# A two-layer edge network on one core: the column sums of the first pass taken by VectorE before one matmul, and a third of a one-column product moved forward

## What is computed

```python
h = maximum(_layernorm(x), 0)
m = concatenate([h[src], bcol[src], edge_attr]) @ W1 + b1      # E x 256, bcol is 0
m = relu(batchnorm(m, g1, be1))                                # statistics over all E rows
agg = segment_sum(m, dst) / maximum(count(dst), 1)             # N x 256
h2 = concatenate([h, bcol, agg]) @ W2 + b2                     # N x 385
h2 = relu(batchnorm(h2, g2, be2))
out = x + relu(h2 @ W3 + b3)
```

## Time and profile before

| | |
|---|---|
| median of 3 runs | 3194.51 us (3186.86 to 3200.58) |
| profiled execution: its own time, its span | 3181.97 us, 3180.2 us |
| busy: PE, PEld | 2441.9 us (77%), 914.3 us (29%) |
| busy: DVE, ACT, POOL | 1393.9 us (44%), 969.7 us (30%), 1749.7 us (55%) |
| first pass, about 145 to 2430 us of the span | 2285 us |
| second pass, about 2430 to 3075 us | 645 us |
| TensorE clock granted, mean | 0.856 |

### The profile page before, as it was taken

How to read it: one execution, slowest core, us unless ns; L and a number is a source line. 1 busy time by engine, 2 the same in 40 slices (tenths; PEclk the granted TensorE clock), 3 DMA queues, 4 the chain that set the end, 5 groups by cost and what they waited for, 6 DMA issues and landing times. The chain is left out here.

```text
span 3180.2 us, 34295 instructions
## 1 busy us (share of the span) xinstructions
PE 2441.9 (77%) x12138; PEld 914.3 (29%) x12138; DVE 1393.9 (44%) x2299; ACT 969.7 (30%) x1601; POOL 1749.7 (55%) x1850
## 2 busy tenths in 40 slices
PE   4666767657767777777777677777867999999998
PEld 3412112112212222222222122222213433444448
DVE  4422212234323333322333233333223899999878
ACT  3322212112212221222122122212213655655546
POOL 6466666666666666666666666666664222222220
PEclk8888778778878888888888888888876999999999
DMA  8466656666656666666666566566664999999965
GB/s 237 155 210 215 212 194 224 209 221 239 216 194 227 212 213 207 218 204 207 216 229 208 190 223 218 195 228 220 212 206 150 337 350 350 345 343 345 341 238 162
DMA packets 270622, 740.85 MB, mean 233 GB/s; under 512 B 46391, under 2 KB 98661, under 8 KB 270448
## 3 DMA queue, kind: packets, MB, share of 16 engines
q1 hardware_dynamic: 189152, 525.28, 46.2%
q0 software_dynamic: 78432, 212.46, 22.4%
q10 hardware_dynamic: 2864, 0.86, 0.1%
HBM read 501.63 MB, written 236.81 MB: 232 GB/s over the span
## 5 line engine op out<-in xcount | busy, mean ns | idle before, releaser
L621 POOL DMA_INDIRECT sums<-P_d,late x1581 | 1496.5, 947 | 796.4 <-issue 453.3
L1052 DVE TENSOR_TENSOR sums<-psum,sums 128x1024 f32<-128x1024 f32 x396 | 479.0, 1220 | 1524.2 <-remote 823.9
L1351 PE MATMUL psum<-late,sums 128*128 128x512 f32 x1660 | 950.3, 687 | 255.2 <-issue 168.4
L709 ACT ACTIVATE sums<-sums 128x1024 f32<-128x1024 f32 x416 | 437.7, 1054 | 1720.7 <-remote 988.0
L1294 PE MATMUL psum<-sums,ones 128*32 128x512 f32 x830 | 486.5, 667 | 117.8 <-issue 70.2
L1351 PEld LDWEIGHTS psum<-late,sums 128*128 128x128 f32 x1660 | 315.4, 210 | 888.6 <-issue 728.0
L1297 PE MATMUL psum<-sums,ones 128*32 128x512 f32 x830 | 497.9, 676 | 59.5 <-issue 58.6
L1296 PE MATMUL psum<-sums,ones 128*32 128x512 f32 x830 | 494.5, 676 | 36.5 <-issue 35.9
L1295 PE MATMUL psum<-sums,ones 128*32 128x512 f32 x830 | 488.7, 670 | 28.8 <-issue 28.6
L1095 DVE TENSOR_TENSOR late<-late,psum 128x1024 f32<-128x1024 f32 (+1 forms) x407 | 482.6, 1212 | 34.3 <-DMA late<-m_d 32.5
L650 POOL TENSOR_TENSOR late<-dst_f,iota 128x384 f32<-128x384 f32 (+1 forms) x139 | 115.1, 829 | 379.4 <-PE psum L1463 375.3
(11 more groups left out here) (215 smaller groups left out, 2012.0 us busy)
## 6 DMA issues: line engine op xcount, KB each, us to landing
m_d<-sums SPq DMA_DIRECT2D x415, 512.0 KB
late<-m_d SPq DMA_DIRECT2D x406, 512.0 KB, 5.5
sums<-in_ea_main SPq DMA_DIRECT2D x103, 512.0 KB
sums<-P_d,late POOLq DMA_INDIRECT x1581
P_d<-sums SPq DMA_DIRECT2D x24, 512.0 KB
nodes<-in_x SPq DMA_DIRECT2D x24, 256.0 KB
late<-in_x SPq DMA_DIRECT2D x24, 256.0 KB, 3.1
out<-late SPq DMA_DIRECT2D x24, 256.0 KB, 2.4
```

What stands on the lines that cost most here:

```text
L621: pool.indirect_dma_start(out=m_s[s][0:r, k * L:(k + 1) * L], out_offset=None, in_=P1_d, in_offset=bass.IndirectOffsetOnAxis(ap=idx[0:r, G ...
L709: act.activation(q_s[g % Q_SLOTS][0:r, 0:w], m_s[g % M_SLOTS][0:r, 0:w], ACT.Square).then_inc(s_q, 1)
L1052: dve.tensor_tensor(m_s[s][0:r, 0:w], ps_m[place_m[g]][0:r, 0:w], m_s[s][0:r, 0:w], ALU.add).then_inc(s_m, 1)
L1351: ins = pe.matmul(ps_m[place_m[g]][:, 2 * i * L:2 * (i + 1) * L], ea[:, i * P:(i + 1) * P], W1c[:, :], start=True, stop=g not in xg_no, sk ...
```

## The change

`stats(g)` of a whole group becomes one matmul. DVE gets `tile_sums(g)`: it sums the four tiles of m to one 128 x 256 tile, and the four tiles of squares to another, side by side, and PE takes the column sums of these 512 columns. `odd_rows(b, 0)` leaves the second pass and stands behind the counts of the first, one block at every other count. Buffers: two for squares instead of three, two new ones for the tile sums; the statistics now lag four groups instead of three. POOL waits for `s_sums` (DVE has read the buffer) instead of `s_st`.

```diff
-Q_SLOTS = 3
+Q_SLOTS = 2
+SUM_SLOTS = 2
+SUM_LAG = 4
...
-    first_odd = [g for g in range(4, FIRST) if g not in init_at]
-    first_odd_at = {g: [b for b in range(NB) if b * len(first_odd) // NB == i] for i, g in enumerate(first_odd)}
...
+        OWN_FIRST, OWN_EVERY = 3, 2
+        own_at = {OWN_FIRST + OWN_EVERY * b: b for b in range(NB)}
...
                 if g >= M_SLOTS:
                     pool.wait_ge(s_mw[s], 16 * (g // M_SLOTS))
-                    pool.wait_ge(s_st, g - M_SLOTS + 1)
+                    pool.wait_ge(s_sums, g - M_SLOTS + 1)
...
                 if g >= Q_SLOTS:
-                    act.wait_ge(s_st, g - Q_SLOTS + 1)
+                    act.wait_ge(s_sums, g - Q_SLOTS + 1)
...
+            def tile_sums(g):
+
+                out = sum_s[g % SUM_SLOTS]
+                if g >= SUM_SLOTS:
+                    dve.wait_ge(s_st, g - SUM_SLOTS + 1)
+                dve.wait_ge(s_m, g + 1)
+                dve.tensor_reduce(out[:, 0:L], m_s[g % M_SLOTS].rearrange("p (t f) -> p f t", f=L), AX.X, ALU.add)
+                dve.wait_ge(s_q, g + 1)
+                dve.tensor_reduce(out[:, L:], q_s[g % Q_SLOTS].rearrange("p (t f) -> p f t", f=L), AX.X, ALU.add).then_inc(s_sums, 1)
...
                 if g in ranges:
                     ranges[g]()
+                if g >= 1:
+                    tile_sums(g - 1)
                 if g in count_at:
                     count_rows(count_at[g])
...
-            dve.tensor_copy(totals, ps_tot[:, 0:L]).then_inc(s_half, 1)
-            dve.wait_ge(s_half, 1)
-            dve.tensor_tensor(totals, totals, ps_tot[:, L:], ALU.add).then_inc(s_tot, 1)
+            dve.tensor_copy(totals, ps_tot[0:SPAN, :]).then_inc(s_tot, 1)
...
             def stats(g):
 
-                pe.wait_ge(s_q, g + 1)
-                r, m, q = rows(g), m_s[g % M_SLOTS], q_s[g % Q_SLOTS]
-                last = GF - 1
                 if g < GF:
-                    pe.matmul(ps_tot[0:32, :], ones[:, 0:32], m[:, 0:2 * L], start=(g == 0), stop=False, skip_group_check=True)
-                    pe.matmul(ps_tot[32:64, :], ones[:, 0:32], m[:, 2 * L:], start=(g == 0), stop=(g == last), skip_group_check=True)
-                    pe.matmul(ps_tot[64:96, :], ones[:, 0:32], q[:, 0:2 * L], start=(g == 0), stop=False, skip_group_check=True)
-                    ins = pe.matmul(ps_tot[96:128, :], ones[:, 0:32], q[:, 2 * L:], start=(g == 0), stop=(g == last), skip_group_check=True)
+                    pe.wait_ge(s_sums, g + 1)
+                    ins = pe.matmul(ps_tot[0:SPAN, :], ones[:, 0:SPAN], sum_s[g % SUM_SLOTS], start=(g == 0), stop=(g == GF - 1),
+                                    skip_group_check=True)
...
+                if q in own_at:
+                    ins = odd_rows(own_at[q], 0)
                 ins.then_inc(s_cnt, 1)
...
-                if g >= 3:
-                    stats(g - 3)
+                if g >= SUM_LAG:
+                    stats(g - SUM_LAG)
...
-                    for b in first_odd_at.get(g, []):
-                        odd_rows(b, 0)
```

More of the change, by code:

```diff
@@ L163, in build @@
         ea_s = [flat[:, 1024 * (M_SLOTS + Q_SLOTS + i):1024 * (M_SLOTS + Q_SLOTS + i + 1)] for i in range(EA_SLOTS)]
+        sum_at = 1024 * (M_SLOTS + Q_SLOTS + EA_SLOTS)
+        sum_s = [flat[:, sum_at + 2 * L * i:sum_at + 2 * L * (i + 1)] for i in range(SUM_SLOTS)]
         assert M_SLOTS >= ROW_SLOTS + 2 and ROW_SLOTS * BN_ <= 2048
@@ L328, in build @@
         ps_bc = psum[:, 3, :]
-        empty_bank = [3 + b % 3 if b < EARLY else 3 for b in range(NB)]
+        empty_bank = [(3, 4, 6)[b % 3] if b < EARLY else 3 for b in range(NB)]
         ps_empty = [psum[:, i, :] for i in empty_bank]
-        ps_odd, ps_bias = psum[:, 6, 0:P], psum[:, 6, 0:KC + 1]
-        ps_n = [psum[:, 4 + i, :] for i in range(2)]
+        ps_odd, ps_bias = psum[:, 5, P:2 * P], psum[:, 5, 2 * P + 8:2 * P + 8 + KC + 1]
+        ps_n = [psum[:, i, :] for i in (4, 6)]
         ps_T = psum[:, 7, 0:L]
@@ L608, in _ @@
             pool.wait_ge(s_pick, 1)
-            for i in range(4):
-                pool.memset(pick[32 * i:32 * i + 1, i // 2:i // 2 + 1], 1.0 / E).then_inc(s_pick, 1)
+            pool.memset(pick[0:1, :], 1.0 / E).then_inc(s_pick, 1)
             pool.wait_ge(s_ei, 48)
@@ new lines, in stats @@
+                    ins = pe.matmul(ps_tot[0:SPAN, :], ones[:, 0:SPAN], sum_s[g % SUM_SLOTS], start=(g == 0), stop=(g == GF - 1),
+                                    skip_group_check=True)
+                else:
+                    r, m, q = rows(g), m_s[g % M_SLOTS], q_s[g % Q_SLOTS]
+                    pe.wait_ge(s_q, g + 1)
+                    pe.matmul(ps_tot[0:SPAN, 0:L], ones[0:r, 0:SPAN], m[0:r, 0:L], start=False, stop=True, skip_group_check=True)
+                    ins = pe.matmul(ps_tot[0:SPAN, L:], ones[0:r, 0:SPAN], q[0:r, 0:L], start=False, stop=True, skip_group_check=True)
@@ L1301, in stats, with odd_rows @@
                 ins.then_inc(s_st, 1)
+            def odd_rows(b, k, start=False):
+                pe.wait_ge(s_oddw, 2 if k else 1)
+                if k:
+                    pe.wait_ge(s_b2, 1)
+                    pe.wait_ge(s_n0, b + 1)
+                v = (nodes, plane[0], plane[1])[k]
+                for t, a, r in tiles_of(b):
+                    ins = pe.matmul(ps_odd[t * SPAN:(t + 1) * SPAN, 0:r], odd_col[:, k, SPAN - 1 - b:2 * SPAN - 1 - b],
+                                    v[:, a:a + r], start=start, stop=(b == NB - 1 and k == KC - 1),
+                                    skip_group_check=True)
+                if k == KC - 1:
+                    ins.then_inc(s_oddacc, 1)
+                return ins
@@ L1368, in _ @@
                     pe.transpose(psum[0:2 * GC, 7, 0:P], rng[:, :], ident[:, :]).then_inc(s_rngT, 1)
-            stats(NG - 3)
-            stats(NG - 2)
-            stats(NG - 1)
+            for g in range(NG - SUM_LAG, NG):
+                stats(g)
             pe.wait_ge(s_tot, 1)
-            pe.wait_ge(s_pick, 5)
+            pe.wait_ge(s_pick, 2)
             pe.wait_ge(s_m, NG)
             for h in range(2):
-                ins = pe.matmul(ps_fin[:, h, :], totals[:, h * P:(h + 1) * P], pick[:, :], start=True, stop=True)
+                for v in range(2):
+                    ins = pe.matmul(ps_fin[:, h, v:v + 1], totals[:, v * L + h * P:v * L + (h + 1) * P], pick[:, :],
+                                    start=True, stop=True)
             ins.then_inc(s_fin, 1)
@@ L1522, in _ @@
                     for k in range(KC):
-                        odd_rows(b, k)
+                        odd_rows(b, k, b == 0 and k == 0)
                     for u in range(3 * KC):
```

33 lines of the change are left out of this document (11 added, 22 removed).

## The result

The changed kernel takes **3487.62 us** (3479.76 to 3502.1), the kernel before beside it 3192.39: a ratio of 1.0932, 95% interval 1.0904 to 1.0961. It is 295 us slower. I had forecast 2972 us with 0.54 for faster; the sign was wrong, though the range held the time.

The account below looks back on a forecast made before the run. The first pass was taken as GpSimd's gather floor of 1971 us plus 314 us waiting on TensorE's lateness. Gains of 214 and 8 us, -222 on 3194.5, gave 2972 us; range 2875 to 3500, the forecast's own 2875 to 3070.

Parts of the forecast that it names:

- floor of 1971 us: First pass, GpSimd: 1581 gathers at 0.947 us plus 0.30 us between two, a minimum time that the change leaves alone.
- the other 314 us: First pass: the rest of its 2285 us, taken as GpSimd waiting, because VectorE is late and itself waits for TensorE.
- if stretches go by instructions, 78 become 48: First pass, TensorE: 78 stretches of slow instruction issue, 10.5 us each, shrink with matmul records, a factor of 0.61.
- 214: First pass: us gained by relieving TensorE, taken between 120 (each remaining stretch delays GpSimd as before) and 314 (none does).
- Rival C: TensorE stays the bound, through stretches going by gathers or time, or the low clock; only 8 us gained, 3187 us; chance 0.06.
- I take 1.20: VectorE's tile sums: us for each of 830 added reductions, priced from rows over neighbouring elements; the ends were 1.20 and 2.29.
- It costs something only when TensorE is within a slow stretch: VectorE's wait for statistics, which TensorE takes one group ahead; it stops VectorE two groups into a stretch instead of three.
- B: VectorE's reductions take 1.92 us, L978's price; VectorE 2272 us, total 3193 us, little or no change; chance 0.17.
- A: The jumping read makes VectorE the bound: 2.29 us a reduction, VectorE 2579 us, total 3500 us, slower; chance 0.27.
- its own point of 1.94: First pass, VectorE: us per reduction from which rival A was said to decide, (2285 - 678) / 830.
- The moved product, -8 us: Head of the second pass: 196 records, 7.9 us on the path, move to the first pass, hidden beside GpSimd.

## Why the prediction was wrong

- *What bounds the kernel.* The floor of 1971 us for the gathers was right: in the quick condition the kernel runs on it. That the other 314 us come from TensorE's lateness fits the record too: it is TensorE's signals that come late. But I took the gaps between TensorE's matmuls for the measure of it.
- *Statistics, "if stretches go by instructions, 78 become 48".* This step failed. With 41% fewer matmuls 73 of 83 stretches stay by the same count, 510 late signals instead of 558, and all that TensorE's relief can win is 21 us, not 214. Rival C held that the stretches need not go by instructions (3187 us), with 0.06; whether they go by time or by gathers stays open.
- *Tile sums, "I take 1.20".* Mis-sized: 1.90 us measured, so 830 x 0.70 = 581 us more work. In the quick condition this alone decides: without the jump the loss is gone. L978's 1.92 us was the right neighbour, and L980's 1.47 was not; nothing in the rows told which. The Trainium skill has a price near it: Vector Engine (DVE) Microarchitecture Reference, Measured stream behaviour on trn2, gives 1.73 ns a column where one of two sources hops at every element and 75 ns fixed, by estimate 1.85 us for 1024; the runs show 1.88 to 1.92. It also says that a single stream alternating between two regions is read at the full rate; the 1.23 us for pairs 512 columns apart agree.
- *"It costs something only when TensorE is within a slow stretch"* (the wait for `s_st`). This step failed as well: taken as some 20 us, measured as 409. Of these 161 need no slow stretch. I had written that the counts are queued behind the new waits, and did not follow the ring on: the count waits for VectorE, the statistics stand behind the count, VectorE waits for the statistics. The order alone is worth 144 us in the quick condition, some 137 in the late. The other 248 us are of the kind that the sentence names, TensorE's late signals, but far more than 20, since VectorE has no idle time left that would hide them.
- *Rivals.* B had the price (1.92 us) and the place of the work (2272 us summed, 2161 found, as VectorE's neighbouring instructions overlap by about 0.1 us), and with 20 us of waits came to 3193. What it lacked were the waits. A named the right direction for a wrong reason: at 1.90 us its own point of 1.94 was not reached. That its 3500 us lie near the measured 3488 is luck, and so is it that the range held the time. The slower side was reached by work just under the pass plus waits, a case that no rival held.
- *The moved product, -8 us.* Right in kind, measured 5.3.

## What to carry to other kernels

Before work goes to an idle engine, write down the ring: who waits for the new work, what that engine has queued ahead of it, and whether one of those waits for the first engine again. An engine's idle time absorbs the lateness of others; here VectorE went from 30% to 84% busy in the stage, and what was left could not. When an engine seems to start late with all its waits done, compare its start with the time at which the semaphore was raised, and not only with the end of the instruction that raises it. Price a jumping read by the rows that jump, not by those that don't, and ask first what the relief on the other side is worth with a kernel that simply leaves the work out.

## What had not been expected

- The same kernel runs in two conditions, 2843 to 2848 us and 3188 to 3212 us, 12% apart, with equal numbers of instruction packets. In the late one many of TensorE's signals come microseconds after the recorded end of their matmuls, 16 us in the case shown, and a good part of the semaphore updates is missing from the trace; in the quick runs signals are prompt and the updates nearly complete. What makes the difference was not found.
- One tensor_reduce over 1024 elements: 1.21 us over neighbours, 1.23 in pairs 2 KB apart, 1.90 in fours 1 KB apart.
- Additions with both operands in SBUF slow GpSimd's gathers: 947 ns become 979 in the mean with one such addition a group and 1041 with four, and only the gathers that overlap an addition are longer.
- TensorE's low clock after an idle stretch doubles the next statistics matmul, 1.04 to 1.91 us, just where VectorE waits for it. This stands in the ring and was removed together with it; its part alone was not measured.
